# Cross attention: the turned group of step 5 in PSUM banks 0 and 1, the value chunk of step 5 in bank 2

## What is computed

```python
q = (x @ Wq + bq); k = (context @ Wk + bk); v = (context @ Wv + bv)   # 16 heads of 16
attn = softmax(einsum('bhld,bhsd->bhls', q, k) * scale)               # 64 x 1601 per head
out = einsum('bhls,bhsd->bhld', attn, v)
x = x + out @ Wo + bo
```

## Time and profile before

| | us |
|---|---|
| median of 3 runs | 4090.07 |
| lowest, highest | 4085.83, 4095.25 |
| the profiled execution | 4096.9 |
| its span in the trace | 4095.6 |
| TensorE busy in it | 3753.1 (92%) |
| VectorE busy | 2759.3 (67%) |
| ScalarE busy | 2150.3 (53%) |
| GpSimd busy | 1459.2 (36%) |

### The profile page before, as it was taken

One profiled execution on the slowest core, in us unless ns is written; L12 is line 12 of the kernel. 1 busy time (PEld: TensorE's weight loads), 2 busy tenths in 40 slices (PEclk: granted clock), 3 DMA queues, 4 the chain that ended last, 5 costly groups with the idle time before them and its releaser, 6 DMA issues. The chain is left out here.

```text
span 4095.6 us, 100177 instructions
## 1 busy us (share of the span) xinstructions
PE 3753.1 (92%) x42032; PEld 3162.9 (77%) x42032; DVE 2759.3 (67%) x7205; ACT 2150.3 (53%) x2963; POOL 1459.2 (36%) x1261
## 2 busy tenths in 40 slices
PE   7999999875999999988999999985997999999857
PEld 6888888634888888757788888864996888888646
DVE  5777777665777777753777777755446777777544
ACT  4565555454655656533455555533654565565434
POOL 3333333101322222130655555403773322222146
PEclk9999999987999999989999999987998999999978
DMA  3122123001111111010211121002542111110035
GB/s 97 50 66 58 50 66 111 25 16 40 42 38 38 42 38 34 18 32 23 77 52 57 50 66 54 30 13 89 196 149 75 38 34 42 42 34 26 13 111 175
DMA packets 125584, 235.80 MB, mean 58 GB/s; under 512 B 9920, under 2 KB 114768, under 8 KB 121296
## 3 DMA queue, kind: packets, MB, share of 16 engines
q1 hardware_dynamic: 118032, 175.58, 14.5%
q0 software_dynamic: 7104, 53.81, 3.8%
HBM read 208.39 MB, written 20.97 MB: 56 GB/s over the span
## 5 line engine op out<-in xcount | busy, mean ns | idle before, releaser
L598 ACT COPY prob_t<-ps 128x1024 f32<-128x1024 f32 x512 | 518.4, 1013 | 1104.5 <-PE ps L486 1104.5
L486 PE MATMUL ps<-c_ident,prob 128*128 128x128 f32 (+1 forms) x6656 | 915.4, 279 | 12.7 <-ACT prob L736 9.9
L486 PEld LDWEIGHTS ps<-c_ident,prob 128*128 128x128 f32 (+1 forms) x6656 | 716.5, 141 | 188.7 <-issue 157.3
L736 ACT ACTIVATE prob<-prob,nmx 128x1601 f32<-128x1601 f32 x512 | 828.7, 1625 | 1.1 <-DVE nmx L649 1.1
L502 PE MATMUL ps<-ctx,wk 128*128 128x400 f32 (+1 forms) x3072 | 692.2, 361 | 21.5 <-DVE vals L608 14.0
L516 PE MATMUL ps<-wv,ctx 128*128 128x256 f32 x4992 | 703.9, 289 | 3.2 <-DVE vals L608 3.1
L516 PEld LDWEIGHTS ps<-wv,ctx 128*128 128x128 f32 x4992 | 619.4, 186 | 10.4 <-DVE vals L608 4.0
L640 DVE CUSTOM_DVE_ANT_0 prob<-ps,mk 128x400 f32<-128x400 f32 (+2 forms) x1024 | 526.7, 570 | 107.9 <-PE ps L474 102.8
L643 DVE TENSOR_SCALAR_CACHE_REDUCE prob<-ps 128x400 f32<-128x400 f32 (+2 forms) x1024 | 526.8, 571 | 92.8 <-PE ps L474 88.7
L502 PEld LDWEIGHTS ps<-ctx,wk 128*128 128x128 f32 x3072 | 535.1, 191 | 45.0 <-DVE vals L608 28.4
L598 DVE COPY prob_t<-ps 128x1024 f32<-128x1024 f32 (+1 forms) x384 | 402.4, 1048 | 246.1 <-PE ps L486 245.7
(11 more groups left out here) (352 smaller groups left out, 4233.6 us busy)
## 6 DMA issues: line engine op xcount, KB each, us to landing
raw_ctx<-in_ctx_t SPq DMA_DIRECT2D x120, 400.0 KB, 3.3
raw_ctx<-in_ctx_t SPq DMA_DIRECT2D x60, 402.0 KB, 5.1
raw_ctx<-in_ctx_t SPq DMA_DIRECT2D x60, 399.0 KB, 3.2
mk<-in_mask_f SPq DMA_DIRECT2D x32, 400.2 KB, 5.5
mk<-in_mask_i SPq DMA_DIRECT2D x16, 800.5 KB, 4.4
sorted<-zeros SPq DMA_DIRECT2D x2, 3840.0 KB, 19.9
rows<-sorted SPq DMA_DIRECT2D x30, 256.0 KB, 3.4
done<-done SPq DMA_DIRECT2D x30, 256.0 KB, 2.4
```

The costliest lines, as they stand in the source:

```text
L486: mm = pe.transpose(ps[0:w, turn_bank(u, i) + a, r * P:(r + 1) * P], prob[u % 2][:, r, x * P:x * P + w], cst['ident'][:])
L598: copy(prob_t[0:w, ring(u, i), 0:nb, :], ps[0:w, turn_bank(u, i):turn_bank(u, i) + nb, :]).then_inc(st[sem], 1)
L736: a.activation(prob[h % 2][:, r, :], prob[h % 2][:, r, :], ACT.Exp, bias=nmx[:, r:r + 1], accum_out=den[h % 2][:, r:r + 1]).then_inc(st['e ...
```

## The change

Two functions that pick a bank answer otherwise for step 5. For every sample but the first, the value chunks 2 and 5 go to bank 2 in place of bank 7. The turned group of step 5 goes to the banks 0 and 1 in place of 4 and 5. (`i == 5` in the last half gave bank 0 before as well.) The waits follow from `free[n]`.

```diff
     def value_bank(b, n):
         if n == 6:
             return TURNED + 1
+        if n in (2, 5) and b:
+            return 2
         return (TURNED, UNIT, TURNED + 1)[n % 3] if b == 0 else UNIT
 
     def turn_bank(u, i):
 
-        return 0 if u == LAST and i % 2 else TURNED
+        return 0 if i == 5 or u == LAST and i % 2 else TURNED
```

## The result

| us | before | after |
|---|---|---|
| median | 4088.03 (4 runs) | 4048.09 (4 runs) |
| lowest, highest | 4085.83, 4095.25 | 4040.44, 4048.89 |
| the profiled execution | 4096.9 | 4040.4 |

The ratio after to before is 0.9895, with a 95% interval of 0.9877 to 0.9913: 1.05% faster, which of 4088.03 us is 43 us (36 to 50 by the interval); the two medians differ by 39.9 us. The forecast was 4059 us, 31 us less, in a range from 4050 to 4068.

A forecast was written before the change was run, and what follows sets the result against it. TensorE's pauses were taken to bound the kernel. The value chunk's 30.6 us plus the turned group's 0.6 us made 31.2 us, taken off the 4090.07 us median: 4059 us, range 4050 to 4068, held at 83%.

The forecast's parts named there:

- What bounds the kernel: Cross attentions: TensorE, busy 727.91 of 738.00 us in the first, sets the time; its pauses are lost time.
- the last half but one: Half 30 of each call: step 6's turned group loses its 0.85 us wait, later waits stay; no gain booked.
- The value chunk's term: Even halves, step 5 values to step 6 keys: 2.46 us falls to 1.95, 0.51 each, 60 times, 30.6 us.
- what that pace is, rows elsewhere show, without a wait between: Odd half, step 3 values to step 4 keys: 2.36 us taken as TensorE's own pace, giving 1.95 with four transposes.
- The check from a second row: Odd half, value chunk 5 to value chunk 6: 1.97 us against 2.46, so 0.49; ends set at 0.46 and 0.53.
- The turned group's term: Step 6's turned group, odd halves: bank 4 free earlier, 0.02 us each, 60 times, 1.2 us; 0.6 us taken.
- the transposes could hardly run sooner anyway: Odd half, step 6's transposes: value chunk's loads run to 321.61, matmuls end later, so only 0.02 us gained.
- What follows and what stays: Behind step 6's keys all moves up 0.51 us; VectorE idle falls 0.86 to 0.35; the fourth exponential does not move.
- Half the gain: Rival, keys' wait for the value copy: only the matmuls' pauses count, 14 us gained, time 4076 us; chance 7%.
- The wait that changes hands: Rival, bank 7 before step 0's keys: VectorE's first pass does not follow, so time is 4089 us; chance 5%.
- the scores that wait for the copies: Rival, head of step 0: scores wait for VectorE's two step 5 copies, slower, 4098 us; chance 3%.
- More than forecast: Rival: keys follow in under 1.95 us or odd halves bring 0.05, 4055 us; below 4050 us chance 2%.

## Why the prediction was wrong, point by point

- **What bounds the kernel: right.** TensorE's pauses were the time, and both waits that the change was said to end ended. Nothing took their place, but for the last half but one (below).
- **The value chunk's term: the mechanism right, the size too small.** It was booked at 0.51 us for an even half and measured 0.62. The step that failed is "what that pace is, rows elsewhere show, without a wait between". The 2.36 us held 0.07 us of waiting for ScalarE's value copy, as both kernels with the keys in bank 3 show. The other 0.04 is in what four transposes less are worth: they were taken at 0.41 us, half of the 0.82 from one group's start to the next, but between 2.29 us with eight and 1.84 us with four lie 0.45. No run takes this 0.04 apart. 60 x 0.11 = 6.6 us were missed here.
- **The check from a second row failed the same way.** The 1.97 us of the odd half were named as holding the wait for bank 4 and then used as an end of the range all the same. The upper end, 0.53, was made from the difference of two rows with a wait in each, so it bounded nothing.
- **The turned group's term: wrong by a factor of ten in the sum.** It was booked at 0.02 us for an odd half, halved in the sum to 0.6 us, and given at most 0.05; it measured 0.11, 6.6 us in all. The failed step is "the transposes could hardly run sooner anyway", argued from the loads' durations: the 12 loads ran to 321.61 and the transposes stood at 321.70. But these loads overlap each other and the next group's too. After the change the turned group's first load is at 296.62, while the value chunk's loads run to 295.23 + 1.47 = 296.70. So the end of the last load does not bound the start of the next one. The start-to-start distance of another pair would have told it: from the values of step 3 to the turned group of step 4 it is 316.06 - 314.64 = 1.42 us, and here it was 1.58. That pair stood in the rows. In all 120 steps 6 of the kernel before the group starts 0.04 to 0.06 us behind the end of VectorE's turned copy, and in the changed kernel 0.11 to 0.14 us ahead of it.
- **The base.** The forecast took its 31.2 us off 4090.07 us, the median of three runs; the median of four is 4088.03. So of the 10.9 us between 4059 and 4048.09, 2.0 are the base's, and the rest the gain's: 39.9 us by the medians, 43.8 by the trace, 31.2 forecast. Off 4088.03 the range would have begun at 4048, and the time would have stood on its edge, with the two terms as wrong as they are.
- **What follows and what stays: right.** VectorE's idle time ahead of L664 fell from 0.86 to 0.25 us; 0.35 were forecast with the smaller gain. The distance from the keys of step 6 to those of step 0 is 299.93 - 297.07 = 2.86 us, as it was. The first turned group of the next half stands at 299.10, and the last exponential ends at 298.42, 0.68 us before. The scores name no releaser but "issue", as before.
- **The last half but one: right.** There the output product and the exponential still set the pace, as these rows of the changed kernel show:

```profile
730.81 0.57 PEld L488 LDWEIGHTS ps<-c_ident,prob 128*65 128x65 f32 x4
...
731.50 0.41 DVE L626 TENSOR_TENSOR X<-ps,X 128x256 f32<-128x256 f32 x1
...
732.03 0.73 PEld L563 LDWEIGHTS ps<-wout,XNT 128*128 128x128 f32 x4 [0.65 <-issue]
732.07 1.10 PE L563 MATMUL ps<-wout,XNT 128*128 128x256 f32 x4 [0.44 <-DVE X L626]
...
733.16 0.85 PEld L488 LDWEIGHTS ps<-c_ident,prob 128*128 128x128 f32 x8 [0.39 <-ACT prob L738]
```

  The turned group lost its wait of 0.85 us and the product behind it waits 0.65 in its place. Its loads stand 0.12 us behind the end of VectorE's addition (731.91), as they did before (742.11 behind 741.99).
- **The rivals.** Half the gain (14 us) fell: the value chunk alone brings 29.7 us, close to the 28.4 by the weight loads and twice the 14.0 by the matmuls' modelled ends. The trace also shows why no load could slip ahead here: the semaphore wait for the value copy stands on the record of the keys' first load itself (300.51), and not on its matmul. The wait that changes hands and the scores that wait for the copies did not come. "More than forecast" is what happened. It had 2% below 4050 us, which leaned on ends that both came from rows with waits in them.
- **A coincidence not to be misread.** The value chunk alone gave 4058.99 us, the number forecast for the whole. It was luck: the prediction had priced one wait about rightly (30.6 us, and this half of the change alone brings 29.7) and the other at next to nothing.

## What to carry to other kernels

Take an engine's own pace only from a pair of rows of which neither waited. To know that, compare the second start with the end of the copy that frees its bank: a start that always stands 0.05 us behind it is a wait. The rows of this profile name no idle time below 0.15 us, and a wait of 0.07 us repeated 120 times is 8 us. Price a wait by start to start against the shortest such distance in the trace, not by the ends of loads or matmuls, which overlap. Where several short-lived buffers share a bank and others lie idle, spread them all: here three bank changes brought 29.7, 13 and 7.5 us one after the other (value chunk, turned group, keys of step 4), each of them a line or two of code.

## What the runs showed of the hardware that was not expected

- A wait that the kernel writes ahead of a matmul holds its weight load too: in the trace the wait stands on the load's record. In the earlier trace rows the keys' first load is 0.06 us behind the copy that frees the bank, and in the changed kernel it starts 0.62 us sooner after its value chunk.
- A late start is in part made good by the group that is late. In the odd half the bank-4 wait held the turned group's start by 0.16 us (1.58 against 1.42 behind the value chunk), but only 0.11 us reached the next group, since the late group was followed sooner (0.39 against 0.44 us from its first load to the next group's).
- It made no difference which banks TensorE wrote beside VectorE's reads. The copy of 128x1024 took 1.22 us out of the banks 0 and 1, with TensorE writing the value chunk into bank 2, and 1.23 us out of 4 and 5, with TensorE writing it into bank 7.
